# Attention values as three fp16 products instead of one fp32 product, with GpSimd making the lower halves

## The reference

```
x  = layernorm(ctx)                 # (32, 1601, 128)
l  = layernorm(latents)             # (32, 64, 128)
q  = l @ Wq ;  k, v = split(concat(x, l) @ Wkv)          # 16 heads of 64
p  = softmax(where(mask, q k^T / 8, -max))               # keys: 1601 context rows, 64 latents
out = layernorm((p v) @ Wout)
```

## Time and profile before

| | us |
|---|---|
| median of three runs | 900.18 |
| the profiled execution's own time | 900.01 |
| its span in the profile | 898.0 |
| TensorE busy | 832.3 (93%) |
| VectorE busy | 594.8 (66%) |
| ScalarE busy | 450.5 (50%) |
| GpSimd busy | 186.5 (21%) |

### The profile page before, as it was taken

The page is one execution under the profiler, slowest core; times in us unless marked ns, Lnnn a source line. Parts: engine busy times, 40 slices in busy tenths (PEclk is TensorE's granted clock), DMA queues, the critical chain, the costliest instruction groups (busy, mean ns, idle before and its releaser), DMA issues.

```text
span 898.0 us, 20741 instructions
## 1 busy us (share of the span) xinstructions
PE 832.3 (93%) x6742; PEld 445.9 (50%) x6743; DVE 594.8 (66%) x1515; ACT 450.5 (50%) x757; POOL 186.5 (21%) x354
## 2 busy tenths in 40 slices
PE   5699999999999999999999999999999999999753
PEld 4344544545454555545454545545454645455522
DVE  5777666666657576766657566766666576747577
ACT  5365454546465545546464545545465554443242
POOL 3011021212122221212222221211222222212101
PEclk9799999999999999999999999999999999999655
DMA  6113221111212121111212111201212111110001
GB/s 204 34 41 103 80 56 40 37 55 52 58 40 54 51 55 54 46 29 52 58 40 55 50 55 55 55 20 52 58 41 59 49 53 53 40 41 17 4 1 47
DMA packets 98347, 45.82 MB, mean 51 GB/s; under 512 B 72100, under 2 KB 90376, under 8 KB 98184
## 3 DMA queue, kind: packets, MB, share of 16 engines
q1 hardware_dynamic: 98256, 45.34, 18.2%
q10 hardware_dynamic: 56, 0.05, 0.0%
HBM read 25.69 MB, written 3.26 MB: 32 GB/s over the span
## 4 chain that ended last, share of the span: by engine, by line
PE 71%; DVE 17%; issue 6%; ACT 3%; DMA 1%; DVEq 1%; POOL 1%; ACTq 0%; SPq 0%; POOLq 0%
PE bank L1299 20%; PE bank L1353 7%; PE bank L1272 6%; PE bank L1227 5%; PE bank L1274 4%; PE bank L1276 4%; DVE mx L1694 4%; PE bank L1244 4%; PE bank L1370 3%; PE bank L1414 3%; DVE xf_all L1723 3%; PE bank L1389 2%; PE bank L1399 2%; PE bank L1243 2%; ACT arena L971 1%
## 5 line engine op out<-in xcount | busy, mean ns | idle before, releaser
L986 ACT ACTIVATE p<-bank,maskbias 128x512 f32<-128x512 f32 x224 | 154.2, 688 | 232.6 <-PE bank L1276 231.1
L1299 PE MATMUL bank<-p,xv 128*128 128x512 f32 (+1 forms) x512 | 238.0, 616 | 0.3 <-POOL arena L840 0.3
L1694 DVE TENSOR_REDUCE mx<-bank 128x1 f32<-128x512 f32 x256 | 165.5, 682 | 53.2 <-PE bank L1244 52.8
L1690 DVE TENSOR_TENSOR qkl_l<-bank,qkl_h 128x512 f16<-128x512 f32 x64 | 41.1, 685 | 76.7 <-ACT qkl_h L974 76.7
L1299 PEld LDWEIGHTS bank<-p,xv 128*128 128x128 f32 (+1 forms) x512 | 74.9, 188 | 31.5 <-issue 23.8
L1272 PE MATMUL bank<-qkc_h,xtT_h 128*128 128x512 f16 (+1 forms) x256 | 86.9, 389 | 0.0
L1244 PE MATMUL bank<-xtT_h,qkc_h 128*128 128x448 f16 x256 | 86.7, 358 | 0.0
L1274 PE MATMUL bank<-qkc_l,xtT_h 128*128 128x512 f16 (+1 forms) x256 | 85.0, 379 | 0.0
L1276 PE MATMUL bank<-qkc_h,xtT_l 128*128 128x512 f16 (+1 forms) x256 | 85.0, 379 | 0.0
L1243 PEld LDWEIGHTS bank<-ltT,qkl_h 128*128 128x128 f16 x256 | 24.9, 97 | 95.4 <-DVE mx L1694 53.9
L1353 PE MATMUL bank<-arena,wvF 128*64 128x128 f32 x1024 | 69.3, 278 | 0.0
(11 more groups left out here) (260 smaller groups left out, 1461.1 us busy)
## 6 DMA issues: line engine op xcount, KB each, us to landing
arena<-den_dram SPq DMA_DIRECT2D x62, 128.0 KB, 3.2
qkc_h<-arena SPq DMA_DIRECT2D x30, 256.0 KB, 2.4
qkc_l<-arena SPq DMA_DIRECT2D x30, 256.0 KB, 2.4
raw<-in_ctx SPq DMA_DIRECT2D x32, 192.0 KB, 2.5
raw<-in_ctx SPq DMA_DIRECT2D x64, 32.0 KB, 2.2
lt<-lt_dram SPq DMA_DIRECT2D x60, 31.8 KB, 2.1
...
```

The costliest lines, as they stand in the source:

```text
L986: a.activation(p32[0:r, slot, :], sbank[t % SRING][0:r, :], ACT.Exp, bias=bias).then_inc(s_probs_ready, 1)
L1299: op = mm(bk[:, :], rows_of[at, :], p32[at, slot, :], start=tile < 2, stop=tile in (0, plan.TILES - 1))
L1694: v.tensor_reduce(mx[:, hq_tile, part:part + 1], bk[:, 0:width], AX.X, ALU.max).then_inc(s_jobs_taken, 1)
```

## The change

- `values` runs three fp16 products: lower rows by upper probabilities, upper by upper, upper by lower. `xv`, `lt` and `p32` hold an upper and a lower fp16 half of each number.
- ScalarE makes each exponential twice: once into the upper fp16 half, once in fp32 into `p_all` (two buffers). GpSimd subtracts the two into the lower half (`low_probs`), at the start of its next step, ahead of everything else in it. `values` waits for that.
- GpSimd makes the context's upper half by its copy and the lower by one more subtraction (XV). The latents' halves are made once (`latents_first` on ScalarE, `latents_low` on GpSimd) and stored to DRAM as halves; their loads have semaphores of their own.
- WINDOW's plan: KEXP 15 to 16, X1B 15 to 17, SHIFT 22 to 23, EXP 23 to 24, MOVE 8 to 11, RDEN of odd halves 3 to 5. KEXP and X1B of the pair before the last come in the drain. In WINDOW the copies of pT out of PSUM (PT_OUT) go from ScalarE to VectorE. ScalarE's EXP comes right behind the exponentials of its step (`self_exp`). TensorE's wait before SC stands behind the values of the step.
- SyncE issues `load_rows` ahead of `rden_rows` in odd halves.

The diff, cut to its core:

```diff
@@ -162,8 +162,8 @@
     EVEN=dict(T=[7.5], MAX=[10.5, 11, 11, 11.5, 12, 12, 12.5, 13], MT=14), XV={2: (0, 4)},
-    RDEN=3, MOVE=8, ST1=[3, 4, 5, 6], YN=[6, 7], XB=7, ST2=8, M0=9, P0=9, X1=10, X1B=15, M1=10, P1=10,
-    XH=12, XHT=13, XHT_OUT=13, QKV=14, QKV_OUT=14, VBLK=15, KEXP=15, SC=16, ALIBI=[17, 18], SMAX=22, SHIFT=22, EXP=23,
+    RDEN=(3, 5), MOVE=11, ST1=[3, 4, 5, 6], YN=[6, 7], XB=7, ST2=8, M0=9, P0=9, X1=10, X1B=17, M1=10, P1=10,
+    XH=12, XHT=13, XHT_OUT=13, QKV=14, QKV_OUT=14, VBLK=15, KEXP=16, SC=16, ALIBI=[17, 18], SMAX=22, SHIFT=23, EXP=24,
     PT=[24, 25], PT_OUT=[24, 25], PV=26, CX=27, CXT=28, CXT_OUT=28, WO=29, X2=30, P2=30, XF=31))
@@ -179,7 +179,7 @@
 BEFORE_LAST = Drain(False, dict(
-    NEVER, SC=0, ALIBI=[1, 1], SMAX=1, SHIFT=2, EXP=2, PT=[5, 5], PT_OUT=[5, 5], PV=6, CX=8, CXT=9, CXT_OUT=9, WO=10, X2=11, P2=12, XF=14))
+    NEVER, KEXP=0, X1B=1, SC=0, ALIBI=[1, 1], SMAX=1, SHIFT=2, EXP=2, PT=[5, 5], PT_OUT=[5, 5], PV=6, CX=8, CXT=9, CXT_OUT=9, WO=10, X2=11, P2=12, XF=14))
 LAST_PAIR = Drain(True, dict(
@@ -327,18 +327,23 @@
         s_xtT_hi = es.enter_context(nc.semaphore("xtT_hi"))
+        s_xv_hi = es.enter_context(nc.semaphore("xv_hi"))
+        s_p_lo = es.enter_context(nc.semaphore("p_lo"))
+        s_lat_hi = es.enter_context(nc.semaphore("lat_hi"))
+        s_lat_lo = es.enter_context(nc.semaphore("lat_lo"))
+        s_lt_loaded = [es.enter_context(nc.semaphore(f"lt_loaded{k}")) for k in range(2)]
         s_xv_ready = es.enter_context(nc.semaphore("xv_ready"))
...
         ltT_dram = nc.dram_tensor("ltT_dram", [2, D, TOK], F16).ap()
-        lt_dram = nc.dram_tensor("lt_dram", [TOK, D], F32).ap()
+        lt_dram = nc.dram_tensor("lt_dram", [TOK, 2 * D], F16).ap()
         den_dram = nc.dram_tensor("den_dram", [2, HQ], F32).ap()
         raw = sb("raw", [P, 2, WHOLE.CH, D], F32)
-        xv = sb("xv", [P, 2, WHOLE.CH, D], F32)
+        xv = sb("xv", [P, 2, WHOLE.CH, 2, D], F16)
         xtT_h = sb("xtT_h", [P, 2, WHOLE.CH * P], F16)
@@ -353,7 +358,7 @@
         ltT = sb("ltT", [P, 2, 2, M], F16)
-        lt = sb("lt", [P, 2, D], F32)
+        lt = sb("lt", [P, 2, 2, D], F16)
         st = sb("st", [P, WHOLE.CH, 6], F32)
@@ -386,11 +391,12 @@
-        aw = words(11008, 4, D)
+        aw = words(10240, 4, D)
         fw = words(8192, 768).rearrange("p (g c n) -> p g c n", g=2, c=3)
...
         lat = xf_all[:, :, :]
+        lat_halves = words(12288, 2048).bitcast(F16).rearrange("p (c h d) -> p c h d", c=PAIRS, h=2)
         ltT_all = x2_all[:, :, :].rearrange("p a b -> p (a b)").bitcast(F16).rearrange("p (j s t) -> p j s t", j=4, s=2)
@@ -403,6 +409,8 @@
         kexp = words(10240, 2, AH // 2, M)
+        p_all = words(11264, 2, HALF)
+        p_halves = p32[:, :, :].rearrange("p a b -> p (a b)").bitcast(F16).rearrange("p (a h b) -> p a h b", a=RING, h=2)
         tsc = words(12288, AH, M)
...
@@ -631,12 +639,14 @@
-                sp.wait_ge(s_lhat_ready, j + 1)
-                sp.dma_start(lt_dram[512 * j:512 * j + 512, 0:127].rearrange("(a p) d -> p a d", p=P), lat[:, block_of(j), 0:127]).then_inc(s_lat_stored, 16)
-                if j == 0:
-                    sp.wait_ge(s_setup_dve, setup_done("lt", 0))
-                else:
+                sp.wait_ge(s_lat_lo, j + 1)
+                sp.dma_start(lt_dram[512 * j:512 * j + 512, :].rearrange("(a p) d -> p a d", p=P),
+                             lat_halves[:, block_of(j), :, :].rearrange("p a h d -> p a (h d)")).then_inc(s_lat_stored, 16)
+                if j > 0:
                     sp.wait_ge(*late_done("lt", j))
+                    store_transposed(j)
+
+            def store_transposed(j):
                 sp.dma_start(ltT_dram[:, :, 512 * j:512 * j + 512].rearrange("s d q -> d s q"), ltT_all[:, j, :, :]).then_inc(s_lat_stored, 16)
...
@@ -678,6 +683,11 @@
                     sp.dma_start(aw[:, k, :], w).then_inc(s_in_aw, 16)
+                store_block(0)
+                for par in range(2):
+                    for half in range(2):
+                        sp.dma_start(lt[M * half:M * half + M, par, :, :].rearrange("p h d -> p (h d)"),
+                                     lat_halves[M * par:M * par + M, 0, :, :].rearrange("p h d -> p (h d)")).then_inc(s_lt_loaded[par], 16)
                 load_rows(plan, None, False, 0)
@@ -703,16 +713,19 @@
                             load_latents(b + 2, par)
-                        if since or k == 1:
+                        if since and k == 0:
                             rden_rows(b - 1, 1 - par, pair)
-                        if since and k == 0:
                             load_x(i - 1)
+                        if more and k == 1:
+                            load_rows(plan, i, last, 1 - par)
+                        if k == 1:
+                            rden_rows(b - 1, 1 - par, pair)
                         if not since and k == 1:
...
                             store_block(3)
-                        if more:
+                        if k == 0:
                             load_rows(plan, i, last, 1 - par)
...
@@ -784,9 +797,24 @@
-                for j, (moments, _, _) in BLOCK_AT.items():
+                for j, (moments, centre, _) in BLOCK_AT.items():
                     if s == moments:
                         latents_rstd(j)
+                    if s == centre + 1:
+                        latents_low(j)
+
+            def latents_low(j):
+
+                pool.wait_ge(s_lat_hi, j + 1)
+                g.tensor_tensor(lat_halves[:, block_of(j), 1, :], lat[:, block_of(j), :], lat_halves[:, block_of(j), 0, :], ALU.subtract).then_inc(s_lat_lo, 1)
+
+            def low_probs(plan, b, k, t):
+
+                r, slot = plan.rows(t), slot_of(plan, k, t)
+                pool.wait_ge(s_probs_ready, b * plan.STEPS + t + 1)
+                if not plan.PAIRED and happened(b * plan.STEPS + t):
+                    pool.wait_ge(s_p_lo, b * plan.STEPS + t)
+                g.tensor_tensor(p_halves[0:r, slot, 1, :], p_all[0:r, t % 2, :], p_halves[0:r, slot, 0, :], ALU.subtract).then_inc(s_p_lo, 1)
@@ -810,7 +838,9 @@
                         g.tensor_copy(maskbias[:, par, 0:CH], mask_bias[plan][:, bass.ds(n, 1), :].rearrange("p o c -> p (o c)")).then_inc(s_maskbias_ready, 1)
-                    op = g.tensor_copy(xv[:, par, c0:c1, 0:127], raw[:, par, c0:c1, 0:127])
+                    g.tensor_copy(xv[:, par, c0:c1, 0, 0:127], raw[:, par, c0:c1, 0:127]).then_inc(s_xv_hi, 1)
+                    pool.wait_ge(s_xv_hi, n * len(at["XV"]) + list(at["XV"]).index(t) + 1)
+                    op = g.tensor_tensor(xv[:, par, c0:c1, 1, 0:127], raw[:, par, c0:c1, 0:127], xv[:, par, c0:c1, 0, 0:127], ALU.subtract)
                     if c1 == CH:
@@ -855,10 +885,16 @@
                     ahead(plan, 1, 1, t)
+                    if t == plan.LAT:
+                        latents_low(0)
...
                         k, t = divmod(s, plan.STEPS)
+                        if t > 0:
+                            low_probs(plan, i * 2 + k, k, t - 1)
+                        elif since or k == 1:
+                            low_probs(plan, i * 2 + k - 1, 1 - k, plan.STEPS - 1)
                         if not (last and k == 1):
...
@@ -910,6 +947,11 @@
+
+            def latents_first(j):
+
+                act.wait_ge(s_lhat_ready, j + 1)
+                a.activation(lat_halves[:, block_of(j), 0, :], lat[:, block_of(j), :], ACT.Copy).then_inc(s_lat_hi, 1)
...
@@ -983,7 +1028,10 @@
                 bias = zrow[0:r, :] if tile == 0 else maskbias[0:r, k, plan.chunk(tile):plan.chunk(tile) + 1]
-                a.activation(p32[0:r, slot, :], sbank[t % SRING][0:r, :], ACT.Exp, bias=bias).then_inc(s_probs_ready, 1)
+                a.activation(p_halves[0:r, slot, 0, :], sbank[t % SRING][0:r, :], ACT.Exp, bias=bias)
+                if happened(gg - 1):
+                    act.wait_ge(s_p_lo, gg - 1)
+                a.activation(p_all[0:r, t % 2, :], sbank[t % SRING][0:r, :], ACT.Exp, bias=bias).then_inc(s_probs_ready, 1)
@@ -1004,6 +1052,16 @@
+
+            def self_exp(plan, p, s):
+                if s == plan.at["EXP"]:
+                    act.wait_ge(s_tsc_shifted, p + 1)
+                    flat = tsc[:, :, :].rearrange("p h k -> p (h k)")
+                    a.activation(flat, flat, ACT.Exp).then_inc(s_sprobs_ready, 1)
+
+            def drained(plan, p, s):
+                self_exp(plan, p, s)
+                tail(plan, p, s)
@@ -1021,17 +1079,13 @@
                     op.then_inc(s_qk_ready, 1)
-                if s == at["EXP"]:
-                    act.wait_ge(s_tsc_shifted, p + 1)
-                    flat = tsc[:, :, :].rearrange("p h k -> p (h k)")
-                    a.activation(flat, flat, ACT.Exp).then_inc(s_sprobs_ready, 1)
                 if plan.own and s in at["HALF_EXP"]:
...
                 for m in range(2):
-                    if s in at["PT_OUT"] and s == at["PT_OUT"][m]:
```

(39 more changed lines are left out.)

23 lines of the change are left out of this document (11 added, 12 removed).

## The result

The changed kernel takes 928.18 us (median of 4 runs, 927.15 to 932.91) against 899.19 us of the kernel before in the same runs. The ratio is 1.0336, with a 95% interval from 1.0294 to 1.0379: 3.4% slower. The forecast of 896.5 us was wrong in sign, and the time lies outside its range.

A forecast was written before the change was run, and what follows sets the result against it. TensorE's instruction order was taken as the bound. Steady pairs: -3.4 +0.8 +0.1 +2.5 = 0.0; first, second and last pairs -5, drain +1.9: -3.1 to -4 us from 900.01, forecast 896.5 us, range 891 to 902.

The forecast's parts named there:

- TensorE's own work: Value products: three fp16 products take 0.65 us instead of 0.86, saving 0.21 per step, 3.4 us per pair.
- The subtraction: GpSimd's subtraction of 128x512 for the lower half: taken as 1.27 us, the nearest row's best two-input add.
- Rival 1: GpSimd's lower halves are the bound, at 1.50 us per subtraction (deciding from about 1.35): 909 us, chance 0.27.
- Steps 8 to 11: Second QL job still starts 7.2 us in; 0.65 us saved is waited away, step 11 begins 0.1 later.
- Steps 11 to 14: Step 14 begins about 0.4 us early, then TensorE waits about 1 us for GpSimd's lower half of step 12.
- The turn of the loop: From step 14 to step 1: late queries (QP 27.8 us in) and GpSimd's KEXP chain make step 1 1.5 us late.
- SC would start there: Turn of the loop: GpSimd's KEXP ends 29.7 us in, and SC starts then, the same point as behind the queries.
- either way: Turn of the loop: query load and GpSimd's chain overlap, so step 1 begins 1.5 us late by each.
- Steps 1 to 8: TensorE saves 7 x 0.21 = 1.5 us; ScalarE's doubled exponentials delay QC copies, costing only 0.1 to 0.2.
- The first pair: First pair of batches, without tail work: keeps about 2 us of the saving.
- The end: Last pair keeps about 2 us; in the drain, exponentials, last lower half and KEXP in sequence add 1.9 us.
- Rival 2: Faster: the savings survive because TensorE takes up slack and half the 3.0 us of waits go: 877 to 880 us, chance 0.23.

The follow-up runs named there:

- e3: Changed kernel with nine unused matmuls of 512 columns ahead of TensorE's wait for the queries: 924.07 us, ratio 1.0264 to the kernel before.
- e1: Changed kernel with SyncE issuing the next pair's query load earlier, in the odd half behind the latents' load: 915.91 us, ratio 1.0169 to the kernel before.
- e7: As e1, with GpSimd's KEXP back from step 16 to 15, ahead of the last lower half: 903.94 us, ratio 1.0049 to the kernel before.
- e12: Changed kernel with GpSimd's subtraction on 64 of 512 columns in the first pair alone: 924.56 us, ratio 1.0286 to the kernel before.
- e11: Kernel before, values in fp32, with only e9's move of VectorE's x_all copy and xf_all behind the next pair's T work: 897.04 us, ratio 0.9962.
- e9: As e7, plus three more queue moves and VectorE's x_all copy and xf_all behind the next pair's T work: 884.21 us, ratio 0.9844 to the kernel before.

## Why the prediction was wrong, by its steps

**TensorE's own work: right.** 0.65 us for three products, and 3.4 us less TensorE work in a pair.

**The subtraction: 1.17 us instead of 1.27.** The row chosen was the nearest one and 0.1 too high. Rival 1 placed its point of decision at 1.35 us and fails as a mechanism: none of the 256 subtractions took over 1.27. Its time (909) is nearer the result than my forecast, but by accident.

**Steps 8 to 11: nearly right.** In a long pair whose step 8 starts at 524.41, the second QL job starts at 531.51, 7.1 in (forecast 7.2), after 0.46 us waited for VectorE (0.65).

**Steps 11 to 14: the place right, the size half.** The wait for GpSimd in step 14 is 0.52 us, not 1, with RSTD ending at 543.94, 19.5 in.

**The turn of the loop: the point of the query load right, what follows it wrong.** QP starts 27.8 in, in the short pair, and 27.7 in the long one (forecast 27.8). Step 1 starts 30.94 in, in the short pair (453.84 against step 8 at 422.90; forecast 30.8 to 31.0), but 32.27 in the long one. **The missing term is the granted clock.** The forecast puts TensorE to 2 us of idle in every pair and then prices what follows at full speed. The length of the wait doesn't tell which pair is hit: 2.02 us ahead of 552.08 was followed by the lower clock, and 2.18 ahead of 450.73 and 2.64 ahead of 246.44 were not. e3 shows that with TensorE kept busy none is. The price is 1.4 us in four pairs, 5.6 us (e3 won 5.1 in them). The pair of 51.2 us ran at 1.00; it is 0.4 longer because its query wait is the one of 2.64 us.

```profile
246.44 0.23 PE L1270 MATMUL bank<-lq,wq_h 128*128 128x128 f16 x1 [2.64 <-DMA lq<-ltT_dram]
450.73 0.23 PE L1270 MATMUL bank<-lq,wq_h 128*128 128x128 f16 x1 [2.18 <-DMA lq<-ltT_dram]
```

The second half of that step, "SC would start there", had the order wrong. TensorE waits for KEXP ahead of QP's second half, not behind it (e1, 1.58 us at 444.77). In the changed kernel this is covered by the query wait. KEXP ends there at 451.22, 28.3 in and not 29.7, because P2 ends 24.2 in and not 25.2. VectorE's xhat does wait for GpSimd, as the walk had it: 1.94 us at 443.43 where it took 1.09 (at 426.10 in the kernel before). So the chains don't cost the same, as the prediction said "either way": e1 took the longer one away and gained 12 us in all, and e7 took 12 more from the other.

**Steps 1 to 8: 0.9 us instead of 1.3 to 1.4.** From step 1 to the next step 8 there are 20.69 us before (434.55 to 455.24) and 19.77 after (453.84 to 473.61). The working had 19.2 to 19.3. TensorE waits 0.60 us at 458.31 for VectorE's QC copies, which come behind ScalarE's doubled exponentials; at the same place of the kernel before (439.21) it stood 0.18. I had "0.1 to 0.2" for that, and left even this out of the sum. The 0.42 us are most of the 0.65 us by which every short pair is longer than before, 9 us in 13 pairs. No run takes the second exponential away, so this cause is read from the trace and not tested.

```profile
458.31 0.20 PE L1300 MATMUL bank<-ltT,qkl_h 128*128 128x64 f16 x1 [0.60 <-DVE arena L1746]
```

**The first pair: the step that failed most.** I gave it a gain of 2 us because it has no tail work, and read no row of it. It lost 10.8. VectorE is busy 35.1 of its 45.9 us in the kernel before (33.1 of 50.05 in a steady pair), so it has less room there, and GpSimd serves latents, rstd and values one after the other. TensorE's waits in that pair, three lines of the changed kernel and then one of the kernel before (us in total, times, longest):

```profile
PE bank L1178 <- DVE xf_all L1593: 5.4, 2, 2.8
PE bank L1359 <- POOL p L817: 3.5, 3, 1.9
PE bank L1300 <- DVE mx L1754: 1.9, 1, 1.9
```

```profile
PE bank L1121 <- DVE xf_all L1533: 2.4, 2, 1.7
```

With the smaller ones they are 11.5 us against 2.9, so 8.6 of the 10.8 stand as waits. e12 takes the full-size subtractions out of that pair alone and wins back 8.4 of the 10.8; its waits there are 5.5 us. One part of that is instructions beside each other: the pair's first four xf_all subtractions take 3.16 us where they took 1.37 us. The Trainium skill (SBUF — State Buffer, "SBUF: two separate sides") has such an exclusion, and the prediction applied it to one xhat of the steady pair; e12's durations agree with it in the first pair, where I didn't look. The traces don't name the mode in which these operations ran. The other part is GpSimd's queue. TensorE's waits for VectorE fell by 3.6 us in e12 and those for the lower halves by 2.4, but how the 8.4 us divide at their source was not measured, since VectorE also waits for GpSimd. Neither is it known what the remaining 2.4 us are. e11's first pair, in which nothing was changed, has the waits of the kernel before and takes 48.6 us, with a granted clock of 0.90 against 0.95; e12's has 0.90 too.

**The end: the drain's number right by luck, the last pair wrong.** From the last mark (the last pair's step 8) to the end it is 2.4 us longer, forecast +1.9. But SC of the pair before the last starts 3.9 us later behind that mark (25.9 us, against 22.0). Some 2 us of that are the forecast chain, TensorE's waits for the last lower halves and KEXP ahead of 853.69. The rest is a wait that no step of the prediction has, 2.85 us for the weights of the feed-forward layer that VectorE prepares (0.17 and 0.24 in the kernel before). Behind SC 1.5 us come back. The 2 us that I let the last pair keep, as I did for the first, are not there either: its first half takes 22.4 us against 22.3, for TensorE waits 2.08 us for KEXP where no query job covers it.

```profile
809.11 1.09 PE L1449 MATMUL bank<-arena,qT 64*64 64x512 f32 x8 [2.08 <-POOL arena L870]
842.38 0.45 PE L1230 MATMUL bank<-identb,fwq 128*128 128x128 bf16 x3 [2.85 <-DVE fwq L1641]
```

Together: 10.8 for the first pair, 0.5 for the second, 9 for the 0.65 us and a little more of every steady pair, 5.6 for the clock, 0.4 for the one longer query wait and 2.5 for the end, less 1.1 at the start, give 27.7 against 27.6. The start is no effect of the change that a run shows: the first mark lies anywhere from 36.6 to 38.1 us in the fourteen traces. Rival 2, with the savings kept, needs that TensorE doesn't wait; e9 shows what that is worth when the queues are mended (884), and it took six moves that the change doesn't have.
